# Feeding float16 values with their rounding offset into the second feed-forward product, in a Perceiver block on one NeuronCore

## The reference

```python
x = x + xattn(layernorm(x), ctx, ctx, mask, Wq, Wk, Wv, Wo)        # 16 heads of 8
x = x + attn(layernorm(x), Wq, Wk, Wv, Wo, W_down_kv, W_up_k, W_up_v)
x = x + ffn(layernorm(x), w1, b1, w2, b2)

def ffn(x, w1, b1, w2, b2):                                        # 128 -> 512 -> 128
    h = qlinear(x, w1, b1)
    h = gelu(h, approximate=False)
    return qlinear(h, w2, b2)

def qlinear(x, w, b):
    sx = max(max(abs(x)), 1e-6) / 127;  xq = round(x / sx)         # one scale for the whole tensor
    sw = max(max(abs(w)), 1e-6) / 127;  wq = round(w / sw)
    return (xq @ wq.T + b) * (sw * sx)
```

## Time and profile before

| | |
|---|---|
| time, median of 3 executions | 331.9 us (331.41 to 331.94) |
| profiled execution: time | 333.19 us |
| profiled execution: span | 331.1 us |
| mean granted TensorE clock | 0.964 |
| busy over the span | TensorE 289.7 us (87%), VectorE 261.3 (79%), ScalarE 257.7 (78%), POOL 231.8 (70%) |
| first product of the feed-forward layer | 290.2 us |
| first product of the second feed-forward product | 315.2 us |
| last output operation ends | 328.35 us |

### The profile page before, as it was taken

How to read it: one execution, slowest core, us unless ns; L and a number is a source line. 1 busy time by engine, 2 the same in 40 slices (tenths; PEclk the granted TensorE clock), 3 DMA queues, 4 the chain that set the end, 5 groups by cost and what they waited for, 6 DMA issues and landing times.

```text
span 331.1 us, 13230 instructions
## 1 busy us (share of the span) xinstructions
PE 289.7 (87%) x5520; PEld 200.8 (61%) x5520; DVE 261.3 (79%) x567; ACT 257.7 (78%) x550; POOL 231.8 (70%) x166
## 2 busy tenths in 40 slices
PE   4796979999999999999889898989898988475784
PEld 2455648676767576776567676756666767221264
DVE  1495668989888788888679796867787999679886
ACT  3485786776769978978798989899878876699592
POOL 5177676875868787789999999999889980073000
PEclk9897999999999999999999999999999999879679
DMA  8996000000000000000000000000000000000026
GB/s 190 244 223 143 3 2 2 4 2 3 5 3 2 4 2 4 4 2 2 2 4 4 4 2 2 4 2 7 2 2 4 2 4 4 2 0 0 0 65 190
DMA packets 19100, 9.51 MB, mean 29 GB/s; under 512 B 5153, under 2 KB 18786, under 8 KB 19042
## 3 DMA queue, kind: packets, MB, share of 16 engines
q1 hardware_dynamic: 18322, 8.25, 11.2%
q10 hardware_dynamic: 720, 0.43, 0.6%
HBM read 6.57 MB, written 2.10 MB: 26 GB/s over the span
## 4 chain that ended last, share of the span: by engine, by line
PE 57%; ACT 20%; DVE 8%; issue 8%; POOL 5%; DMA 1%; ACTq 0%; DVEq 0%; POOLq 0%
PE ps L548 10%; PE ps L529 8%; PE ps L575 7%; PE ps L591 5%; PE ps L581 5%; ACT arena L846 4%; ACT vx L736 4%; PE ps L462 4%; PE ps L453 3%; ACT pt L770 3%; PE ps L469 3%; PE ps L546 2%; ACT arena L763 2%; POOL ud L372 2%; PE ps L435 2%
## 5 line engine op out<-in xcount | busy, mean ns | idle before, releaser
L770 ACT ACTIVATE pt<-ps 128x512 f32<-128x512 f32 x128 | 75.9, 594 | 20.0 <-PE ps L548 19.5
L380 POOL TENSOR_TENSOR u<-u,mx 128x1024 f32<-128x1024 f32 x32 | 60.9, 1904 | 39.1 <-DVE mx L977 38.9
L372 POOL TENSOR_TENSOR ud<-u,con 128x1024 f32<-128x1024 f32 x31 | 73.5, 2371 | 2.4 <-DVE u L963 2.2
L958 DVE SCALAR_TENSOR_TENSOR u<-ps,rs,arena 128x1024 f32<-128x1024 f32 x32 | 41.0, 1282 | 19.2 <-PE ps L529 19.1
L963 DVE TENSOR_SCALAR u<-ps 128x1024 f32<-128x1024 f32 x32 | 39.1, 1221 | 18.5 <-PE ps L529 16.4
L529 PE MATMUL ps<-arena,qT 32*64 32x256 f32 x1024 | 44.9, 408 | 6.4 <-ACT arena L763 4.3
L380 POOL TENSOR_TENSOR ud<-ud,mx 128x768 f32<-128x768 f32 x30 | 44.2, 1474 | 2.4
L575 PE MATMUL ps<-pt,vx 128*32 128x64 f32 x2048 | 41.4, 222 | 2.5 <-DVE oT L904 2.1
L575 PEld LDWEIGHTS ps<-pt,vx 128*32 128x32 f32 x2048 | 32.5, 111 | 16.0 <-issue 10.1
L763 ACT ACTIVATE arena<-kT,cst,con 128x512 f32<-128x512 f32 x51 | 41.5, 817 | 0.3
L581 PE MATMUL ps<-pt,con 128*32 128x128 f32 x1024 | 40.0, 275 | 0.0
(11 more groups left out here) (148 smaller groups left out, 545.3 us busy)
## 6 DMA issues: line engine op xcount, KB each, us to landing
out<-pt SPq DMA_DIRECT2D x8, 256.0 KB, 2.3
x<-in_x SPq DMA_DIRECT2D x4, 256.0 KB, 3.7
arena<-in_ctx SPq DMA_DIRECT2D x8, 128.0 KB, 4.0
x<-in_x SPq DMA_DIRECT2D x2, 512.0 KB, 6.2
arena<-in_ctx SPq DMA_DIRECT2D x4, 256.0 KB, 6.5
arena<-in_mask_BxS_if SPq DMA_DIRECT2D x2, 256.0 KB, 4.9
arena<-in_mask_BxS_if SPq DMA_DIRECT2D x4, 64.0 KB, 4.1
arena<-in_mask_BxS_if SPq DMA_DIRECT2D x2, 128.0 KB, 3.6
```

The lines of the kernel that those rows point to most:

```text
L372: pool.tensor_tensor(dh, uh, decay.unsqueeze(1).to_broadcast([P, H, HALF]), ALU.mult)\
L380: pool.tensor_tensor(uh, uh, mx[:, n % 4, 0:count].unsqueeze(2).to_broadcast([P, count, HALF]), ALU.subtract)\
L770: act.activation(pt[:, n % 2, 4 * half:4 * half + 4].rearrange("p h n -> p (h n)"), ps[:, bank, :], ACT.Exp).then_inc(s["emptied"], 1)
L958: dve.scalar_tensor_tensor(by_head(u[:, n % UB]), sc, rs[:, 0, n:n + 1], mask[:, n].unsqueeze(1).to_broadcast([P, H, HALF]), ALU.mult, ALU ...
```

## The change

The offset 1536 is no longer subtracted on VectorE. The float16 values go into the product as they are, and TensorE takes the offset out again: the bank of each group is opened with `-1536 * w2q` summed over the 512 hidden units, four products of a 128x128 tile of -1536 (`minus_off`) with the chunks of `w2qT`, repeated for the four tiles. Seven banks are opened before the reduction (which moves to bank 7) and the eighth after it. The bias enters in a closing product per group: its three bf16 parts stand in rows 0, 32 and 64 of a tile `b2q` of 96 rows, else zero, and `ones_b` has 96 rows. POOL clears the tile, ScalarE copies the rows in at turn 24.

VectorE's order is now a list, `DVE_TAIL`: "a" rounds a group, "f" makes its output. Group 6 moves from ScalarE to VectorE, and VectorE rounds group 0 in two halves; TensorE starts on its first two tiles after the first. The ring `hq` is gone.

The rounding of w2 writes w2q in its own order, and reads w2r with a step of four elements.

```diff
-H_ACT = (1, 2, 4, 5, 6, 7)
+H_ACT = (1, 2, 4, 5, 7)
+DVE_TAIL = (("a", 0), ("a", 3), ("f", 0), ("f", 1), ("a", 6)) + tuple(("f", g) for g in range(2, 8))
...
-        ones_b = sb("ones_b", [1, P], BF16)
+        b2q = sb("b2q", [96, D], BF16)
+        ones_b = sb("ones_b", [96, P], BF16)
+        minus_off = sb("minus_off", [P, P], F16)
...
                 pool.memset(ones_b[:, :], 1.0)
+                pool.memset(minus_off[:, :], -ROUND16)
+                pool.memset(b2q[:, :], 0.0).then_inc(s["b2_zero"], 1)
...
-            def bias(g):
-                for c in range(3):
-                    pe.matmul(ps[:, g, :], ones_b[:, :], b2h[:, c].unsqueeze(1).to_broadcast([1, GT, D]),
+            def offset(g):
+
+                for c in range(FC):
+                    pe.matmul(ps[:, g, :], minus_off[:, :], w2qT[:, c].unsqueeze(1).to_broadcast([P, GT, D]),
                               start=(c == 0), stop=False)
-            pe.wait_ge(s["b2_split"], 5)
-            for g in range(6):
+            pe.wait_ge(s["b2_placed"], 3)
+            for g in range(7):
                 if g % 2 == 0:
                     pe.wait_ge(s["gelu_done"], 13 + g // 2)
-                bias(g)
+                offset(g)
             pe.wait_ge(s["hred_local"], 1)
-            pe.transpose(ps[0:1, 6, 0:P], scal[:, 16:17], ident).then_inc(s["hred_row"], 1)
+            pe.transpose(ps[0:1, 7, 0:P], scal[:, 16:17], ident).then_inc(s["hred_row"], 1)
             pe.wait_ge(s["hred_max"], 1)
             pe.matmul(ps[:, 7, 0:1], ones_row[0:1, :], row[:, 1:2], start=True, stop=True).then_inc(s["hred_all"], 1)
             for g in range(NG):
-                if g == 2:
+                if g == 0:
                     pe.wait_ge(s["hscale"], 1)
-                    bias(6)
-                    bias(7)
-                pe.wait_ge(s["hq_ready"], g + 1)
+                    offset(7)
+                if g in H_ACT:
+                    pe.wait_ge(s["hr_done"], H_ACT.index(g) + 1)
+                else:
+                    pe.wait_ge(s["hr_done_dve"], (1 if g == 0 else 1 + sum(e not in H_ACT for e in range(g + 1))))
                 for i in range(GT):
+                    if g == 0 and i == 2:
+                        pe.wait_ge(s["hr_done_dve"], 2)
                     for c in range(FC):
-                        last = pe.matmul(ps[:, g, i * P:(i + 1) * P], hq[:, g % 4, c, i * P:(i + 1) * P],
-                                         w2qT[:, c], start=False, stop=(i == GT - 1 and c == FC - 1))
-                last.then_inc(s["down_done"], 1)
+                        pe.matmul(ps[:, g, i * P:(i + 1) * P], h16[g % 6][:, c, i * P:(i + 1) * P],
+                                  w2qT[:, c], start=False, stop=False)
+                pe.matmul(ps[:, g, :], ones_b[:, :], b2q[:, :].unsqueeze(1).to_broadcast([96, GT, D]),
+                          start=False, stop=True).then_inc(s["down_done"], 1)
...
-                    act.activation(w2q[:, :, :].rearrange("o c p -> o p c"),
-                                   w2r[:, :].rearrange("o (p c) -> o p c", c=FC), ACT.Identity, bias=cst[:, 4:5])\
+                    act.activation(w2q[:, :, :], w2r[:, :].rearrange("o (p c) -> o c p", c=FC), ACT.Identity, bias=cst[:, 4:5])\
...
+                if n == 24:
+                    act.wait_ge(s["b2_zero"], 1)
+                    act.wait_ge(s["b2_split"], 5)
+                    for c in range(3):
+                        act.copy(b2q[32 * c:32 * c + 1], b2h[:, c]).then_inc(s["b2_placed"], 1)
...
                 if g >= 6:
-                    act.wait_ge(s["hq_ready"], g - 5)
+                    act.wait_ge(s["down_done"], g - 5)
...
-                    dve.tensor_scalar(hq[:, g % 4], h16[g % 6], -ROUND16, None, ALU.add)\
-                        .then_inc(s["hq_ready"], 1)
...
+            for what, g in DVE_TAIL:
+                if what == "a":
+                    if g >= 6:
+                        dve.wait_ge(s["down_done"], g - 5)
+                    parts = 2 if g == 0 else 1
+                    width = GT * P // parts
+                    for part in range(parts):
+                        cols = slice(part * width, (part + 1) * width)
+                        dve.tensor_scalar(h16[g % 6][:, :, cols],
+                                          hidden[:, :, g * GT * P + part * width:g * GT * P + (part + 1) * width],
+                                          scal[:, 19:20], ROUND16, ALU.mult, ALU.add).then_inc(s["hr_done_dve"], 1)
+                else:
+                    dve.wait_ge(s["down_done"], g + 1)
                     if g >= 4:
-                        dve.wait_ge(s["down_done"], g - 3)
+                        dve.wait_ge(STORED[g % 4], 16)
```

More of the change, by code:

```diff
@@ L198, in perceiver_block @@
         x16 = [u[:, g // 4].bitcast(F16)[:, g % 4 * GT * P:(g % 4 + 1) * GT * P] for g in range(NG)]
-        hq = vx[:, :, :, :, :, :, :].rearrange("p j b t r c m -> p (j b t r c m)")[:, 0:4096].bitcast(BF16) \
-            .rearrange("p (s c n) -> p s c n", s=4, c=FC)
         ob = pt[:, :, :, :].rearrange("p s h n -> p (s h) n")
@@ L211, in perceiver_block @@
             filled emptied
-            b2_split kx_made kx_pool kx_first s_done s_read maxed maxed16 clipped decayed shifted decayed_dve shifted_dve
+            b2_split b2_zero b2_placed kx_made kx_pool kx_first s_done s_read maxed maxed16 clipped decayed shifted decayed_dve shifted_dve
             pv_done ln_done den_ready o_ready wo_done x_added
@@ L215, in perceiver_block @@
             amax_done ared_local ared_row ared_max ared_all ascale xr_done xr_done_act xr_done_pool xq_ready xq_ready_pool up_done gelu_done
-            hmax_done hred_local hred_row hred_max hred_all hscale hr_done hr_done_dve hq_ready
+            hmax_done hred_local hred_row hred_max hred_all hscale hr_done hr_done_dve
             down_done ob_ready stored0 stored1 stored2 stored3""".split()
@@ L1039, in _ @@
             dve.wait_ge(s["hred_row"], 1)
-            dve.tensor_reduce(row[:, 1:2], ps[0:1, 6, 0:P], AX.X, ALU.max).then_inc(s["hred_max"], 1)
+            dve.tensor_reduce(row[:, 1:2], ps[0:1, 7, 0:P], AX.X, ALU.max).then_inc(s["hred_max"], 1)
             dve.wait_ge(s["hred_all"], 1)
@@ L1047, in _ @@
             dve.wait_ge(s["hscale"], 3)
[L1048 to L1056, removed]
-                    if g >= 4:
-                        dve.wait_ge(s["down_done"], g - 3)
-                    dve.tensor_scalar(hq[:, g % 4], h16[g % 6], -ROUND16, None, ALU.add)\
-                        .then_inc(s["hq_ready"], 1)
[L1061 to L1068, removed]
@@ new lines, in _ @@
+            for what, g in DVE_TAIL:
[11 more added lines that the diff above has]
+                    dve.wait_ge(s["down_done"], g + 1)
+                    if g >= 4:
+                        dve.wait_ge(STORED[g % 4], 16)
+                    dve.scalar_tensor_tensor(ob[:, (g % 4) * GT:(g % 4 + 1) * GT].rearrange("p t d -> p (t d)"),
+                                             ps[:, g, :], scal[:, 20:21],
+                                             x[:, g * GT:(g + 1) * GT].rearrange("p t d -> p (t d)"),
```

## The result

The changed kernel took 328.87 us, median of 4 (328.19 to 330.19), beside 331.92 for the kernel before (331.41 to 334.81). The ratio is 0.9885, with a 95% interval of [0.9842, 0.9929]: 0.7 to 1.6% faster. The forecast was 328.9 us in a range of 328.1 to 330.6. So the forecast of the changed kernel's time held. Medians and ranges hold all executions; the ratios leave out those more than 1.5% above the fastest of the same kernel.

The account below looks back on a forecast made before the run. The prediction took the tail to be paced by VectorE at about 1.25 us a group, with a low clock and a w2q stall. Terms -2.3 (tail) and -0.7 (w2q copy) gave -3.0 from 331.9: 328.9 us, range 328.1 to 330.6.

Parts of the forecast that it names:

- The w2q copy, -0.7: First layer: adjacent writes cut ScalarE's w2q copy from 2.60 to 0.8 us, removing TensorE's stall, -0.7 us.
- Rival 1: First layer: the w2q copy stays long, only the tail's gain counts, 329.6 us; chance 0.20.
- The copies of the bias and the memsets, 0: ScalarE's three bias copies (at most 0.75 us) and POOL's memsets hide in idle time; cost 0.
- The opening products, +0.6 at the scale: Before the reduction: 28 products of 128 rows take 6.16 us; VectorE's scale comes 0.6 us later, bounds +0.45 and +0.7.
- Scale to last output, -2.9 in the prediction's steps (-2.3 with +0.6 at the scale): Tail: groups cost TensorE 1.12 us at full clock; last output operation starts at 325.3 instead of 327.60, -2.3 us.
- rival 4: Tail: mixed float16 and bf16 products run at half speed, TensorE is the bound, 333.8 us; chance 0.03.
- The clock: From 306 us to the end: 128-row products keep the granted clock at 1.00, where one-row products lost it.
- The starting point: Whole kernel: the 3.0 us gain is taken from 331.9 us, the median of the unprofiled runs.
- rivals 2 and 3: Clock falls in the opening products, 332.6 or some 339.5 us, chance 0.07; or only after, 329.3 or 331.2, 0.10.

Follow-up runs that it names:

- the kernel before filled on both sides: Kernel before with 128-row bias products, six extra before the reduction and nine directly behind the scale; 330.65 us beside 333.24, ratio 0.9943.
- the second series: The changed kernel unchanged, timed again in five rounds beside the kernel before: 328.89 us beside 333.82, ratio 0.9869.

## Why the prediction was right, and where it was off

**The w2q copy, -0.7: right.** It took 1.25 us in the changed kernel, where I had taken 0.8, between the bounds of 0.74 and 2.60 and under the 1.89 at which TensorE begins to wait. The turn took 3.36 us where I had expected 3.37, and the old copy put back cost 0.74 to the first GELU. Between the traces before and after only 0.16 of it arrived, as the clock fell earlier ahead of the GELUs. Of the cacheline rule in the Trainium skill (SBUF — State Buffer, "Door 1: The DMA port swizzle") these runs show the penalty: a read four fp32 apart took 0.5 us more than the adjacent one, for 512 elements. They don't show the free stride of four fp32 that the same note gives. The scattered bf16 write cost 1.9 us. Rival 1 asked for a copy above 1.89 us and is out.

**The copies of the bias and the memsets, 0: right.** Three copies took 0.92 us, more than the 0.75 that I had as a bound, and three memsets 0.2 us each. The turns behind both kept their length (3.83 us from turn 25 on, 3.82 before).

```profile
114.76 0.92 ACT L835 COPY b2q<-b2h 1x128 bf16<-1x128 bf16 x3
```

**The opening products, +0.6 at the scale: too high by 0.3.** The 28 took 6.20 us where 6.16 was expected, and the transpose came 20.54 us after the first GELU instead of 19.96, +0.58 and not +0.70. The reduction behind it, at the full clock, took 1.06 us instead of 1.36; I had allowed 0.1 of that. Together the scale came 0.28 us later, outside my bounds of +0.45 and +0.7. (The forecast's own range, 328.2 to 329.6, is also wider than these bounds and the 0.4 for handovers make it: 328.75 to 329.4.)

**Scale to last output, -2.9 in the prediction's steps (-2.3 with +0.6 at the scale): right.** It measured -2.90. The first product started 1.25 us behind the scale, and sixteen mixed products and the bias of 96 rows came every 1.12 us. The mean of a mixed product is 219 ns. That of an unmixed one, in the kernel before filled on both sides, where the clock was full too, is 220:

```profile
L665 PE MATMUL ps<-w2qT,ud 128*128 128x128 bf16 x64 | 4.4, 219 | 0.7 <-ACT ud L866 0.7
L663 PE MATMUL ps<-w2qT,vx 128*128 128x128 bf16 x128 | 8.4, 220 | 3.6 <-DVE vx L1065 3.6
```

So rival 4 is out. TensorE waited ahead of groups 2 and 5, as worked out, for 0.66 and 0.46 us. With group 5 on VectorE the second wait was gone, and the tail was 0.64 us shorter.

**The clock: right, and worth more than the sum had it.** The opening with one row brought the old fall back, and in the kernel before 128 rows took it away from the opening products. Of the tail's 2.62 us, 1.23 came when the clock was held up (36.27 to 35.04). Part of that can be the six products that open banks 6 and 7: they moved ahead of group 0, and in the trace before group 2 had followed them without a wait. The other 1.39 us are the rest of the change: no subtraction, the new order, and a first product 1.25 us behind the scale instead of 2.52. No run takes these apart.

These sizes hold for the one trace of the kernel before. In the trace with the new w2q copy the old tail was 2.5 us longer at the lower clock. The times of the kernel before go with its clock. Of the 60 executions in the three later series that the ratios use, the 14 with a mean clock of 0.969 took 331.7 to 334.7 us, the 18 with 0.956 to 0.958 took 333.7 to 335.7, and the 8 with 0.948 took 336.1 to 336.8. The mean doesn't say in which stage the clock was low, so how much of the 4.9 us between the medians of the second series is the tail's stays open.

**The starting point: weak, and the closeness is luck.** That 328.87 us met 328.9 to 0.03 is no merit of the sum. I took 3.0 us from 331.9, the median of three executions, and didn't ask how steady the kernel before was. From the 333.19 us of the traced execution, which gave the rows, the same sum makes 330.2, within the range but 1.3 us above the 328.93 of the changed kernel's. Of the 4.26 us between the two traced executions the stages that I priced gave 2.76, the clock near 30 us 1.24, and the time outside the span the rest. Inside the 2.76, two misses partly cancelled: 0.54 us less than expected ahead of the first GELU, 0.32 more at the scale. I had weighed a clock that falls or stays low for the changed kernel (rivals 2 and 3) and not for the one before, whose clock was low in the tail by the earlier trace rows.

On the clock the Trainium skill (TensorE: Matmul & The Clock Gate, "What's actually happening") ties it to how busy the engine is. The runs agree for gaps: with 128-row bias products it fell when TensorE had been busy 0.65 of 2.60 us ahead of the first product. They disagree for one-row products, which came back to back and lost the clock in three traces.

## What to carry to other kernels

Read the clock row by stages before pricing anything on TensorE: here products of one row let the clock fall to half, for themselves and for what came behind them, and the same products padded with zero rows kept it. When a stage waits for a chain of small steps (a reduction over partitions), the clock can fall in the gaps, and filling them is worth a trial: with both sides of the chain filled the one trace kept the clock, though the times don't set this apart from the zero rows alone. And when a kernel's times spread, compare stages of traces, from one fixed event to the next, since medians of a few executions can hide 0.7 us and show 2.

## What the runs showed of the hardware that I had not expected

A product whose rows are all but one zero kept the clock at 2.4 GHz (18 in 4.04 us); with one real row alone it fell to 1.2 GHz 2.4 to 3.3 us after the first. The clock's return differed as much: at 318.5 us in one trace of the old tail, 3.3 us after its dense products had begun, and only after 324 us in another, where the six one-row products stood between (that they delayed it is my reading; no run tested them alone, though with these six 128 rows high the clock came back at 320.1 us, 4.5 us after the dense products had begun). On ScalarE, 512 elements a partition took 0.74 us read and written side by side, 1.25 read as fp32 four apart, and 2.60 written as bf16 128 apart. Whether the write cost more as a write or for its longer step no run shows. The clock also fell near 30 us in six of twelve traces, in old and new kernels alike, at a price of 1.3 us in the pair above.
